# A language-model tower on one core: half of the small transfers that place the softmax maxima move to GpSimd's queue, and the maxima run 11 steps ahead of the scores in place of 13

## The reference

```python
h = tok(x)                                # table rows, softmax over 64 clusters, coarse rows
h = h + attn(layernorm(h))                # 8 heads of 16, softmax(q k^T) v, silu, w_o
h = h + ffn(layernorm(h))                 # router to 2 of 64 experts, capacity 128, FFN of 512
```

## Time and profile before

| | us |
|---|---|
| median of 3 runs | 1194.92 |
| lowest and highest run | 1194.0, 1200.92 |
| the profiled execution, its own time | 1192.67 |
| its span in the trace | 1190.9 |

### The profile page before, as it was taken

How to read it: one execution, slowest core, us unless ns; L and a number is a source line. 1 busy time by engine, 2 the same in 40 slices (tenths; PEclk the granted TensorE clock), 3 DMA queues, 4 the chain that set the end, 5 groups by cost and what they waited for, 6 DMA issues and landing times. The chain is left out here.

```text
span 1190.9 us, 30565 instructions
## 1 busy us (share of the span) xinstructions
PE 1019.2 (86%) x12144; PEld 537.1 (45%) x12144; DVE 983.6 (83%) x2004; ACT 762.0 (64%) x1414; POOL 220.5 (19%) x321
## 2 busy tenths in 40 slices
PE   0586674749999999999999999999999849897978
PEld 0474563612434444444444344444444225856556
DVE  4679798868899889989999989989898357879794
ACT  0357665722787788888888788888878935152432
POOL 6776858330000000000000000000000010202020
PEclk9976775755999999999999999999999987989899
DMA  3232857780243242432424233242300241313011
GB/s 71 69 106 95 177 124 89 159 211 7 38 79 51 41 89 38 64 66 49 81 38 73 57 55 56 58 72 38 72 12 12 89 135 38 97 53 115 8 35 36
DMA packets 81841, 85.04 MB, mean 71 GB/s; under 512 B 24241, under 2 KB 58614, under 8 KB 81718
## 3 DMA queue, kind: packets, MB, share of 16 engines
q1 hardware_dynamic: 70710, 73.87, 28.3%
q0 software_dynamic: 2560, 5.25, 3.3%
q10 hardware_dynamic: 8448, 4.20, 1.2%
HBM read 48.78 MB, written 34.08 MB: 70 GB/s over the span
## 5 line engine op out<-in xcount | busy, mean ns | idle before, releaser
L1089 DVE TENSOR_REDUCE b_neg_max<-psM 128x1 f32<-128x1024 f32 x512 | 603.3, 1220 | 67.3 <-PE psM L987 64.1
L1061 ACT ACTIVATE prob<-psS 128x512 f32<-128x512 f32 x1024 | 529.1, 604 | 157.5 <-PE psS L1007 157.5
L987 PE MATMUL psM<-ks,qs 96*32 96x512 bf16 x4096 | 416.0, 394 | 18.2 <-PEq L850 14.4
L1007 PE MATMUL psS<-qs,ks 99*32 99x512 bf16 x4096 | 404.9, 382 | 6.5 <-ACT prob L1061 4.5
L1021 PE MATMUL psO<-prob,vs 128*17 128x512 f32 x2048 | 266.4, 592 | 0.2 <-ACT prob L1061 0.2
L1007 PEld LDWEIGHTS psS<-qs,ks 99*32 99x32 bf16 x4096 | 114.0, 96 | 208.4 <-ACT prob L1061 103.1
L987 PEld LDWEIGHTS psM<-ks,qs 96*32 96x32 bf16 x4096 | 113.4, 97 | 176.9 <-DVE b_neg_max L1089 83.4
L882 POOL CAST mpart<-b_neg_max 128x16 bf16<-128x16 f32 x32 | 6.3, 196 | 635.1 <-DVE b_neg_max L1089 622.0
L322 POOL DMA_INDIRECT emb<-in_table,idx x80 | 79.5, 994 | 34.0 <-issue 18.3
L1021 PEld LDWEIGHTS psO<-prob,vs 128*17 128x17 f32 x2048 | 59.5, 98 | 52.0 <-ACT prob L1061 1.1
L1285 ACT ACTIVATE y_t<-c_psT 128x512 f32<-128x512 f32 x16 | 9.6, 597 | 87.6 <-PE c_psT L1345 87.6
(11 more groups left out here) (130 smaller groups left out, 1058.0 us busy)
## 6 DMA issues: line engine op xcount, KB each, us to landing
qk_parts<-qk_part SPq DMA_DIRECT2D x48, 256.0 KB, 3.4
qs<-qk_parts SPq DMA_DIRECT2D x192, 64.0 KB, 3.6
ks<-qk_parts SPq DMA_DIRECT2D x96, 128.0 KB, 4.3
o_cols<-ot SPq DMA_DIRECT2D x32, 256.0 KB, 4.5
qs<-mpart_t SPq DMA_DIRECT2D x384, 1.0 KB, 1.7
v_rows<-vrow SPq DMA_DIRECT2D x16, 272.0 KB, 9.6
vs<-v_rows SPq DMA_DIRECT2D x8, 544.0 KB, 5.1
h_rows<-h SPq DMA_DIRECT2D x16, 256.0 KB, 4.3
```

Source lines behind the costliest of these rows:

```text
L987: last = nc.tensor.matmul(psM[count % MRING][q * HP:(q + 1) * HP, n, :], qs[buf][0:DATA_ROWS, half, hh, at + q * HP:at + (q + 1) * HP], ks ...
L1007: last = nc.tensor.matmul(psS[unit % SRING][q * HP:(q + 1) * HP, :], ks[buf][0:ROWS, GH * gb + hh, tile * P + q * HP:tile * P + (q + 1) * HP],
L1061: nc.scalar.activation(prob[step % PRING][:, hh, :], psS[unit % SRING][:, :], ACT.Exp).then_inc(score_free, 1)
L1089: nc.vector.tensor_reduce(neg_max[e % 2][:, unit:unit + 1], psM[count % MRING][:, :, :], AX.XY, ALU.max, negate=True).then_inc(max_free, 1)
```

## The change

`LEAD` goes from `TOKT + 5` = 13 to `TOKT + 3` = 11. The 12 transfers of a set are divided: SP keeps the six of the quarters 0 and 1, and GpSimd gets the six of the quarters 2 and 3 in a new function `place_upper`, which follows the split of the same set in its program and waits for the same transposition. They count on a semaphore of their own, `upper_loaded`, one for each parity, and PE waits for both. `PLACES`, the number of transfers that PE waits for on each semaphore, goes from 12 to 6.

```diff
@@ -797,12 +797,12 @@
     STEPS = HALVES * TOKT
     PAIR = 2 * GROUPS * STEPS
     PAIRS = BATCH // 2
-    LEAD = TOKT + 5
+    LEAD = TOKT + 3
     SRING, MRING, PRING = 3, 2, 4
     HTILES = TOKT // HALVES
     M_STEP = MAXES // TOKT
     SETS = 2 * GROUPS * HALVES
-    PLACES = PARTS * (P // HP)
+    PLACES = PARTS * (P // HP) // 2
     SPLITS = 4
 
     ctx = ExitStack()
@@ -841,6 +841,7 @@
         split = sem("split")
         max_t_done = sem("max_t_done")
         max_loaded = [sem(f"max_loaded{i}") for i in range(2)]
+        upper_loaded = [sem(f"upper_loaded{i}") for i in range(2)]
         out_free = sem("out_free")
         o_stored = [sem(f"o_stored{i}") for i in range(2)]
         sums_loaded = sem("sums_loaded")
@@ -887,11 +888,23 @@
                     pool.wait_ge(split, k + 3)
                     nc.gpsimd.tensor_tensor(mpart[i][:, 2, :], mrest[i][:, :], mpart[i][:, 1, :], ALU.subtract).then_inc(split, 1)
 
+                def place_upper(n):
+
+                    buf, gb, half = n // (GROUPS * HALVES) % 2, n // HALVES % GROUPS, n % HALVES
+                    pool.wait_ge(max_t_done, n + 3)
+                    for a in range(P // HP // 2, P // HP):
+                        for m in range(PARTS):
+                            dst = qs[buf][DATA_ROWS + m:DATA_ROWS + m + 1, half, GH * gb:GH * (gb + 1), :]
+                            dst = dst.rearrange("o h (t a r) -> o a (h t) r", a=P // HP, r=HP)[:, a, :, :]
+                            row = a * HP + m * MAXES % HP
+                            pool.dma_start(dst, mpart_t[n % 2][row:row + MAXES, m * MAXES // HP, :]).then_inc(upper_loaded[n % 2], 16)
+
                 pool.wait_ge(stores_landed, 1)
                 nc.gpsimd.memset(ks[1][DATA_ROWS:ROWS, :, :], 1.0).then_inc(cleared[1], 1)
                 pool.wait_ge(cleared[1], 1)
                 for n in range(BATCH * SETS // 2):
                     split_maxima(n, n % 2)
+                    place_upper(n)
 
             @block.sync
             def _(sp):
@@ -899,7 +912,7 @@
 
                     buf, gb, half = e // (GROUPS * HALVES) % 2, e // HALVES % GROUPS, e % HALVES
                     sp.wait_ge(max_t_done, p * SETS + e + 3)
-                    for a in range(P // HP):
+                    for a in range(P // HP // 2):
                         for n in range(PARTS):
                             dst = qs[buf][DATA_ROWS + n:DATA_ROWS + n + 1, half, GH * gb:GH * (gb + 1), :]
                             dst = dst.rearrange("o h (t a r) -> o a (h t) r", a=P // HP, r=HP)[:, a, :, :]
@@ -999,6 +1012,7 @@
                         if e % (SETS // 2) == 0:
                             pe.wait_ge(cleared[buf], 1)
                         pe.wait_ge(max_loaded[e % 2], (p * (SETS // 2) + e // 2 + 1) * 16 * PLACES)
+                        pe.wait_ge(upper_loaded[e % 2], (p * (SETS // 2) + e // 2 + 1) * 16 * PLACES)
                     for hh in heads:
                         unit = step * GH + hh
 
```

## The result

The changed kernel takes 1230.03 us (median of 4 runs, 1225.69 to 1232.98) against 1195.15 before: a ratio of **1.0288**, interval 1.0264 to 1.0313. It is slower by about 35 us, where 190 were forecast.

A forecast was written before the change was run, and what follows sets the result against it. PE alone was taken to set the pace. The profiled 1192.67 + 132 (waits) - 3 (old waits) + 62 (clock) - 0.3 (start) + 0.7 (end) = 1384; with 2.25 to the median, 1385 us was forecast, range 1215 to 1445.

The forecast's parts named there:

- The margin: From a set's first transfer issue to its first score: 9.4 us, falling to 4.2 with two steps less lead.
- SyncE's six: SP's transfers in each set: sixth lands 5.2 us after first issue, 1.0 us late, 31 us over 31 sets.
- GpSimd's six: GpSimd's transfers in each set: sixth lands at 8.45 us, so PE stands still 4.25 us a set, 132 us.
- a beat of 1.1: Time from one GpSimd transfer issue to the next, in us, taken somewhat below the gather's 1.24.
- for the landing I take 2.65: Us from GpSimd's last issue to its landing: 0.94 issue, 1.1 as for SP's transfers, 0.6 on top.
- The lower end, SyncE's beat: Lower bound for GpSimd's transfers: SP's beat and landing, late by 1.0 us a set like SP's.
- The 0.6 for contention: Us added to GpSimd's landing because SP's next loads start behind six transfers and run beside GpSimd's last ones.
- The clock's 62 us: PE's waits of 4.25 us bring half-clock stretches in most sets, costing 2.0 us a set.
- The start of the stage: Before the first score: two steps less save 4.7 us, but set 0's wait for GpSimd's half leaves 0.3.
- SP's half ends last: Rival: GpSimd issues near SP's beat; sets late by 1.0 us, no clock fall, 1218 us; chance 0.16.

The follow-up runs named there:

- twelve a set: All twelve transfers on GpSimd at lead 13: 1212.56 us; the same with SyncE's next loads held until they land: 1192.96 us.
- twelve transfers on SyncE: The kernel before with only the lead shortened to 11, all transfers staying on SyncE: 1409.97 us, ratio 1.1772.
- five and seven: The changed kernel at lead 11 with five transfers on SyncE and seven on GpSimd: 1245.49 us, ratio 1.0444.
- SyncE's six alone: The changed kernel at lead 11 without GpSimd's six transfers, and PE's wait for them, from the ninth set on: 1221.27 us, ratio 1.0232.

## Why the prediction was wrong

**The margin** was right: 9.4 us less two beats. The unhindered distance at lead 13 is 9.66 us in the divided kernel too, and all the waits fit 4.44. (The waits of the kernel before, taken as 3 us, were 4.1. The last addition of the sum is off by one, 1384 and 2.25 make 1386; it changes nothing.)

**SyncE's six** were forecast to land 5.2 us after the first issue and late by 1.0 a set. Measured, without set 21 the sets are late by (38.6 - 5.7) / 30 = 1.1 on average, so the size was right, though it is made of 0.6 to 1.0 in twenty sets and of 1.6 to 2.2 in the ten with an instruction read, which I had not seen. With these six alone the kernel loses 27.7 us, all gains counted.

**GpSimd's six are the step that failed**, "a beat of 1.1" and "for the landing I take 2.65". The beat is 0.484 and the landing 1.5 to 1.6, so the half lands 0.53 + 5 x 0.484 + 1.5 = 4.5 us after the transposition instead of 8.7, before SyncE's. Where the sum had 132 us of waits, 34.5 were measured, most of them SyncE's. I took the gather as the nearest row because engine and queue were the same. Its 0.94 us belongs to 128 indices and 64 KB; a direct transfer of 16 runs costs half. The lower end, SyncE's beat, was itself too high. The 0.6 for contention was the right mechanism and did not apply: with six and six the loads are issued at 4.0 us after the transposition, but their first data move at 5.2, when GpSimd's last transfer has landed (4.5). Where they start sooner it is larger than I had it, 2.7 us at the median.

**The clock's 62 us** followed from the same error. The size per fall was right (2.0 against 2.1, and 31 falls of 31 where the scores were late by 4.4 to 5.8 us), but all pauses but one were under 2 us and only two falls came, some 3 to 4 us.

**The start of the stage** gave 3.2 us; I had 0.3 with GpSimd's half last and 3.6 in the rival. That rival, "SP's half ends last", was the true case with 0.16; its 1218 us misses GpSimd's one long stop (4.7 us over the others), the 3 to 4 us of the clock and some 2 us of the waits; a further 5 us of the profiled execution lie behind the last set's first score. It had no chance higher because a price that no row showed was taken from the costlier neighbour, and the bound from below was not asked for its own reasons: the trace had no direct transfer of GpSimd at all, which should have left the two cases near even.

The Trainium skill, "Perfetto Trace Analysis", section DMA Optimizations, says that spreading transfers over the issuing engines may help where descriptor generation bounds. The traces agree: dividing them takes the last landing from 9.4 us after the transposition to 5.1, and is worth 0.4% at lead 13. The Trainium skill, "DMA: Bandwidth & Descriptors", Specifications, gives GpSimd's way 1 us to the first byte and SyncE's 0.6. The landings in a set without a read beside them, counted from the start of the issue, are 1.5 us for GpSimd's 1 KB and 1.7 for SyncE's, so for a transfer of this size GpSimd's way is no later.

## What to carry to other kernels

Count a wait from the margin: the time from the release of a transfer to the work that needs it, less the time to its landing. Cutting the lead by two steps here took 5.2 us of margin and the divided issue returned 4.3, so the sum was a loss; one step, 2.6, was paid for, and that kernel was faster by 0.3%. Where two queues carry the halves of one job, ask what each does next, for a queue that gets done sooner starts its large loads sooner, beside the other's small transfers. And a price that no row shows should be run by itself before the change is built on it.

## What was new about the hardware

- A direct transfer of 1 KB (16 runs of 64 bytes, SBUF to SBUF) takes GpSimd 484 ns to issue, less than SyncE's 589, with nothing between two of them; twelve in a row take 5.76 us. It lands 1.5 us after the start of its issue. The gathers of the same kernel take 944 ns with 0.30 between.
- Beside loads of 64 and 128 KB the same transfers landed 4.2 us after issue at the median (at most 5.7).
- One 16 KB instruction read for PE, about 1.0 us long, delays the small transfers beside it by 1 to 1.5 us: SyncE's sixth issue came late in the six sets with the read at 1.5 to 2.9 us after the transposition, its landing in the four with the read at 3.2 to 4.0. By which path it does so is not shown.
- GpSimd's issue of direct transfers stood still for 2.91 us before the 129th in six kernels, and for 2.5 us before the 129th, 249th and 369th in the two with twelve a set.
- Each of PE's 31 pauses with twelve transfers on SyncE (4.0 to 5.6 us) had the granted clock at 0.50 from its last part or right behind it (174 us in all), and so did 30 of the 31 at a lead of 10 (2.4 to 8.7 us; 201 us). Of the ten pauses of 1.4 to 1.9 us in the changed kernel one did. Near 2 us it went either way: with five and seven, pauses of 2.0 and 2.3 us did and one of 2.2 did not, nor did one of 2.3 with SyncE's six alone.
